# Attention softmax: the VectorE queue of a step is put into another order

## The chip, the cores and the metric

The kernel runs on one core of a Trainium2 chip. The metric is the device time of one execution of the whole program in microseconds (us); less is better. TensorE multiplies, VectorE (DVE in the profile) does reductions and elementwise work and reads PSUM, ScalarE (ACT) evaluates functions and copies out of PSUM, GpSimd (POOL) does elementwise work in SBUF alone. Each engine works through its own queue in program order, and the queues meet at semaphores.

## The reference, cut to what matters

The program computes six layers on a residual stream x of 8 x 256 tokens x 128 channels: a small graph of FFN nodes, the attention layer, the FFN graph again, a mixture of experts, a state-space layer and a second mixture. Only attention is touched by the change:

```python
xn = (x - mu) / jnp.sqrt(var + 1e-05) * ln_gamma + ln_beta
q, k, v = jnp.split(xn @ w_qkv, 3, axis=-1)      # 16 heads of 64
def rotate(t):
    t1, t2 = (t[..., :half], t[..., half:])
    return jnp.concatenate([t1 * cos - t2 * sin, t2 * cos + t1 * sin], axis=-1)
qr, kr = (rotate(q), rotate(k))
scores = jnp.einsum('bhid,bhjd->bhij', qr, kr) * scale
probs = jax.nn.softmax(scores, axis=-1)
out = jnp.einsum('bhij,bhjd->bhid', probs, v)
out = out.transpose(0, 2, 1, 3).reshape(b, n, INNER)
return out @ w_out + b_out
```

## The kernel before

Attention (`attn_phase`) is cut into 32 units: 8 sequences (b) times 4 groups of four heads (p). A loop of 37 steps runs a software pipeline over them, the same loop in the queue of each engine. In step s, unit f = s is projected and rotated, unit m = s - 2 goes through scores and softmax, unit t = s - 3 through the transposes and the product with v, and unit o = s - 4 through the output projection and the addition to x. Step s - 5 names z, of which only the last group of a sequence matters: there `moments` takes mean and variance of the finished x, in one step of four.

TensorE's order in a step: `scores` (L843), transposes of heads 0 and 1 (`turn`, L855), `project_out` (L881), first projection (`project(f, 0)`, L817), transposes of heads 2 and 3, `values` (L828), second projection (`project(f, 1)`, L817 again), `context` (L871). The two projections share one PSUM bank, `proj`, so that `project(f, 1)` waits until VectorE has done `rotate(f, 0)`, and the next unit's `project(f, 0)` until `rotate(f, 1)` is done. Both are two multiplications of `proj` by the tables into `turned` (L920). `values` waits for `add(o)` (L960), which reads the same bank `vc`. The next step's `scores` waits for the fourth exponential (`pr_sb`), since that one reads the last of the score banks.

VectorE's softmax work: `row_max` is a reduction of one head's scores (L929), `negate` turns the maxima of two heads into the bias of the exponentials (L935), `invert` takes the reciprocal of the sums of two heads once their exponentials are done (L941), and `normalize` multiplies the four tiles of heads 0 and 1 (L948). GpSimd does the sums and differences of the rotation (`rot`, L1009 and L1011) and the multiplication of heads 2 and 3 (L1018), in the order first rotation, multiplication, second rotation; the multiplication waits for the second `invert`.

ScalarE's order in a step: two copies of transposes (`pt`, L1043), exponentials of heads 0 and 1 (L1058, two per head, each with a read of the sum), two more copies, the copy of v (L1084, waits for `values`), exponentials of heads 2 and 3, the copy of the context (L1050). The exponentials of heads 2 and 3 wait for `negate` of the second pair.

VectorE's order is written out by hand in the step loop that the diff changes. No planner and no DMA has a part in it.

Of the kernel before, what the change touches and what calls it, by code (L numbers as in the profile page):

```python
# [8 lines left out]
ALU = mybir.AluOpType  # L9
ACT = mybir.ActivationFunctionType  # L10
AX = mybir.AxisListType
# [731 lines left out]
QUADS = HA // 4  # L743
HALF = DA // 2
UNITS_A = B * QUADS
SOFT_LAG, TURN_LAG, PROJ_LAG = 2, 3, 4
# [12 lines left out]
def attn_unit(step, lag):  # L759

    return Unit(step - lag) if 0 <= step - lag < UNITS_A else None
# [16 lines left out]
def attn_phase(k, a):  # L778

    nc, d = k.nc, k.d  # L780
    wqk, wv, wo, rope, bo = a.wqk, a.wv, a.wo, a.rope, a.bo
    with ExitStack() as ctx:
# [3 lines left out]
        mx = k.sb("at_mx", [P, 2, 8], ctx)  # L786
# [8 lines left out]
        sc = [k.psum(f"at_sc{h}", [P, 2, N], ctx) for h in range(4)]  # L795
# [5 lines left out]
        s = {n: k.sem(f"at_{n}", ctx) for n in names}  # L801
# [110 lines left out]
        @block.vector  # L912
        def _(dve):
            def rotate(f, which):

                dve.wait_ge(s["proj_ps"], 2 * f.n + which + 1)
                if f.n:
                    dve.wait_ge(s["rot_sb"], 4 * f.n - 2 + 2 * which)
                for i in range(2):
                    last = nc.vector.tensor_tensor(turned[:, which, i, :, :], proj[:, :, :],  # L920
                                                   rope[:, i:i + 1, :].broadcast_to([P, 2, N]), ALU.mult)
                last.then_inc(s["rope_sb"], 1)

            def row_max(m, pair):

                if pair == 0:
                    dve.wait_ge(s["sc_ps"], m.n + 1)
                for h in (2 * pair, 2 * pair + 1):
                    last = nc.vector.tensor_reduce(mx[:, m.two, 2 * h:2 * h + 2], sc[h][:, :, :], AX.X, ALU.max)  # L929
                last.then_inc(s["mx_sb"], 1)  # L930

            def negate(m, pair):

                dve.wait_ge(s["mx_sb"], 2 * m.n + pair + 1)
                nc.vector.tensor_scalar(nmx[:, m.two, 4 * pair:4 * pair + 4], mx[:, m.two, 4 * pair:4 * pair + 4], -scale,  # L935
                                        None, ALU.mult).then_inc(s["nmx_sb"], 1)

            def invert(m, pair):

                dve.wait_ge(s["pr_sb"], 4 * m.n + 2 * pair + 2)  # L940
                nc.vector.reciprocal(rinv[:, m.two, 4 * pair:4 * pair + 4], rsum[:, m.two, 4 * pair:4 * pair + 4])\  # L941
                    .then_inc(s["rinv_sb"], 1)

            def normalize(m):

                dve.wait_ge(s["rinv_sb"], 2 * m.n + 1)
                for i in range(4):
                    last = nc.vector.tensor_scalar(pr[:, m.two, i, :], pr[:, m.two, i, :], rinv[:, m.two, i:i + 1],  # L948
                                                   None, ALU.mult)
                last.then_inc(s["pn01_sb"], 1)  # L950

            def add(o):

                dve.wait_ge(s["op_ps"], o.n + 1)
                if o.n:
                    dve.wait_ge(s["x_sb"], o.n)
                else:
                    dve.wait_ge(s["bias"], 1)
                xs = k.x[:, 2 * o.b:2 * o.b + 2, :]
                nc.vector.tensor_tensor(xs, xs, vc[:, 0, :].rearrange("p (t d) -> p t d", t=2), ALU.add)\  # L960
                    .then_inc(s["x_sb"], 1)

            def moments(b):

                dve.wait_ge(s["x_sb"], QUADS * (b + 1))
                for i in range(2):
                    nc.vector.bn_stats(stx[:, b % 2, i, :], k.x[:, 2 * b + i, :]).then_inc(s["stx_sb"], 1)
                for i in range(2):
                    dve.wait_ge(s["stx_sb"], 2 * b + i + 1)
                    nc.vector.bn_aggr(k.mv[:, 2 * b + i, :], stx[:, b % 2, i, :])  # L970

            front.invert(dve)
            for b in range(2):
                front.center(dve, b)
            dve.wait_ge(a.loaded, 16 * (len(a.loads) + 1))
            for step in steps:
                f, m, o = attn_unit(step, 0), attn_unit(step, SOFT_LAG), attn_unit(step, PROJ_LAG)
                if m:
                    row_max(m, 0)
                    negate(m, 0)  # L980
                    row_max(m, 1)
                if o:
                    add(o)
                z = attn_unit(step, PROJ_LAG + 1)
                if z and z.p == QUADS - 1:
                    moments(z.b)
                if m:
                    negate(m, 1)
                if f:
                    rotate(f, 0)  # L990
                if m:
                    invert(m, 0)
                if f:
                    rotate(f, 1)
                if step == 0:
                    for b in range(2, B):
                        front.center(dve, b)
                if m:
                    invert(m, 1)
                    normalize(m)  # L1000

        @block.gpsimd
        def _(pool):
# [1103 lines left out]
```

## Time and profile before

| | |
|---|---|
| runs, median of 3 | 2348.8 us (2347.6 to 2350.88) |
| profiled execution, time | 2348.22 us |
| its span | 2346.5 us |
| TensorE busy | 2108.6 us, 90% |
| VectorE busy | 1750.2 us, 75% |
| ScalarE busy | 1373.3 us, 59% |
| GpSimd busy | 997.3 us, 43% |
| attention, first scores to the last addition | 566.9 to 880 us |

The span is the time between the first and the last recorded instruction; the execution's own time is 1.7 us longer. Busy shares are means over all layers. For a change in one layer, the stretch of that layer is to be read, and there the length of a step, from one `scores` to the next.

### The profile page before, as it was taken

The page shows a single profiled execution, that of the slowest core. Times are in us where ns is not written, and L with a number is a line of the kernel's source. Part 1 is how long each engine was busy: PE and PEld are TensorE (multiplying, and loading weights), DVE is VectorE, ACT ScalarE, POOL GpSimd, SP SyncE. Part 2 cuts the span into 40 slices and gives each one's busy share as a digit, 9 for nine tenths or more (in the row PEclk, how much of TensorE's full clock was granted, in tenths as well). Part 3 has the DMA queues.
Part 4 walks back from the last instruction along what each step waited for, and adds up shares of the span by engine and source line. Part 5 has one row for each costly group of instructions (what it writes and reads, how often), then busy time and mean ns, then how long its engine had stood idle before and what let it go on. Part 6 is the DMA issues. An engine that isn't in the chain of part 4 may idle for free. (4 is left out here: it accounts for less than half of the span.)

```text
span 2346.5 us, 41150 instructions
## 1 busy us (share of the span) xinstructions
PE 2108.6 (90%) x14740; PEld 1526.7 (65%) x14740; DVE 1750.2 (75%) x3007; ACT 1373.3 (59%) x2711; POOL 997.3 (43%) x1461
## 2 busy tenths in 40 slices
PE   4899999986999985999999979699999999999978
PEld 3566666654777763666666645486776776866745
DVE  5666666666777767666666665499999999999963
ACT  1566666674777762666666663467567576575433
POOL 2444444523776654444445403033343333333313
PEclk7899999997999996999999998899999999999979
DMA  5555555530000004455555504000000000000000
GB/s 164 128 137 132 136 137 135 132 73 1 2 1 2 2 1 107 131 133 134 133 138 133 132 25 178 1 1 1 1 1 1 1 1 1 1 1 1 1 14 18
DMA packets 147459, 144.77 MB, mean 62 GB/s; under 512 B 14272, under 2 KB 107072, under 8 KB 146368
## 3 DMA queue, kind: packets, MB, share of 16 engines
q1 hardware_dynamic: 147264, 142.22, 23.0%
q8 instruction: 116, 1.90, 0.4%
q14 instruction: 79, 0.65, 0.1%
HBM read 93.94 MB, written 38.80 MB: 57 GB/s over the span
## 5 line engine op out<-in xcount | busy, mean ns | idle before, releaser
L604 DVE TENSOR_REDUCE sb_f_mx<-ps_f_s 128x2 f32<-128x512 f32 x768 | 504.6, 687 | 286.7 <-PE ps_f_s L360 285.6
L534 ACT ACTIVATE sb_f_pt<-ps_f_t 128x1024 f32<-128x1024 f32 x384 | 390.6, 1020 | 91.6 <-PE ps_f_t L377 91.2
L1959 POOL TENSOR_TENSOR sb_mb_h<-sb_mb_h 128x512 f32<-128x512 f32 x128 | 165.9, 1317 | 490.6 <-DVE sb_mb_h L1819 490.6
L360 PE MATMUL ps_f_s<-sb_f_stack 96*128 96x256 bf16 x1536 | 287.2, 279 | 54.8 <-DVE sb_f_mx L604 27.2
L1814 DVE TENSOR_TENSOR_SCAN sb_mb_h<-sb_mb_da,sb_mb_h 128x1024 f32<-128x1024 f32 x128 | 291.0, 2312 | 2.1 <-ACT sb_mb_da L1678 2.1
L1527 PE MATMUL ps_mb_f<-sb_mb_fc,sb_mb_cw 128*128 128x256 f32 x1280 | 285.3, 380 | 2.0 <-ACT sb_mb_fc L1692 2.0
L1527 PEld LDWEIGHTS ps_mb_f<-sb_mb_fc,sb_mb_cw 128*128 128x128 f32 x1280 | 240.2, 190 | 37.2 <-ACT sb_mb_fc L1692 4.3
L1678 ACT ACTIVATE sb_mb_da<-sb_mb_dl,sb_mb_an 128x255 f32<-128x255 f32 x512 | 211.4, 495 | 54.9 <-DVE sb_mb_h L1814 39.4
L712 POOL CAST sb_f_parts<-sb_f_qf 128x512 bf16<-128x512 f32 x96 | 58.5, 609 | 425.2 <-ACT sb_f_qf L561 425.2
L377 PE MATMUL ps_f_t<-sb_f_stack 128*128 128x256 bf16 x1536 | 234.7, 275 | 1.5 <-ACT sb_f_pt L534 1.5
L360 PEld LDWEIGHTS ps_f_s<-sb_f_stack 96*128 96x128 bf16 x1536 | 140.9, 99 | 105.2 <-DVE sb_f_mx L604 66.9
L433 PE MATMUL ps_f_a<-sb_f_pt,sb_f_v 128*32 128x256 f32 x3072 | 186.6, 384 | 0.0
L377 PEld LDWEIGHTS ps_f_t<-sb_f_stack 128*128 128x128 bf16 x1536 | 142.3, 98 | 59.7 <-issue 38.7
L545 ACT ACTIVATE sb_f_cs<-ps_f_a 128x512 f32<-128x512 f32 x96 | 57.3, 597 | 179.7 <-PE ps_f_a L433 179.7
L1819 DVE TENSOR_TENSOR sb_mb_h<-sb_mb_h,ps_mb_c 128x1024 f32<-128x1024 f32 x128 | 148.6, 1200 | 2.6 <-PE ps_mb_c L1563 2.6
L1807 DVE TENSOR_TENSOR sb_mb_h<-ps_mb_b,sb_mb_dx 128x1024 f32<-128x1024 f32 x128 | 150.0, 1211 | 0.5
L433 PEld LDWEIGHTS ps_f_a<-sb_f_pt,sb_f_v 128*32 128x32 f32 x3072 | 90.4, 110 | 82.6 <-issue 33.5
L1018 POOL TENSOR_SCALAR sb_at_pr<-sb_at_pr,sb_at_rinv 128x256 f32<-128x256 f32 x128 | 120.0, 952 | 50.2 <-DVE sb_at_rinv L941 50.2
L1058 ACT ACTIVATE sb_at_pr<-ps_at_sc,sb_at_nmx 128x256 f32<-128x256 f32 x256 | 118.3, 486 | 5.0 <-DVE sb_at_nmx L935 4.1
L716 POOL TENSOR_TENSOR sb_f_r<-sb_f_qf,sb_f_parts 128x512 f32<-128x512 f32 x96 | 112.5, 1172 | 7.7
L721 POOL TENSOR_TENSOR sb_f_parts<-sb_f_r,sb_f_parts 128x512 bf16<-128x512 f32 x96 | 111.8, 1164 | 7.7
L920 DVE TENSOR_TENSOR sb_at_turned<-ps_at_proj,sb_at_rope 128x512 f32<-128x512 f32 x128 | 82.2, 683 | 43.4 <-PE ps_at_proj L817 43.4
(256 smaller groups left out, 4209.9 us busy)
## 6 DMA issues: line engine op xcount, KB each, us to landing
f_scr<-sb_f_parts SPq DMA_DIRECT2D x96, 384.0 KB, 2.8
sb_f_stack<-f_scr SPq DMA_DIRECT2D x192, 192.0 KB, 3.1
sb_f_stack<-f_scr SPq DMA_DIRECT2D x192, 128.0 KB, 3.1
sb_f_stack<-f_scr SPq DMA_DIRECT2D x192, 64.0 KB, 3.3
sb_f_stack<-sb_f_mrow SPq DMA_DIRECT2D x96, 96.0 KB
sb_mb_cw<-in_cw SPq DMA_DIRECT2D x1, 5120.0 KB, 19.9
sb_m_w<-in_w SPq DMA_DIRECT2D x6, 256.0 KB, 3.1
sb_prep_weT<-in_weT SPq DMA_DIRECT2D x1, 1152.0 KB, 7.3
```

What stands on the lines that cost most here:

```text
L360: last = nc.tensor.matmul(s_bank[j % 2][:, h, :], stack[0:ROWS, a.n % STACKS, 0, g * GROUP + pair * 2 + h, half * P:(half + 1) * P], stack ...
L377: last = nc.tensor.matmul(t_bank[i % 2][:, h, :], stack[:, e.n % STACKS, 1, g * GROUP + h, half * P:(half + 1) * P], stack[:, e.n % STACKS ...
L433: last = nc.tensor.matmul(act_bank[h * SLOT:(h + 1) * SLOT, g * N:(g + 1) * N], v[:, u.two, half, g * GROUP + h, :], pt[:, u.two, g, half, ...
L534: nc.scalar.activation(pt[:, e.two, g, half, :, :], t_bank[i % 2][:, :, :], ACT.Exp).then_inc(s["pt_sb"], 1)
L604: nc.vector.tensor_reduce(mx[:, a.two, half, head:head + 2], s_bank[j % 2][:, :, :], AX.X, ALU.max)\
L1018: last = nc.gpsimd.tensor_scalar(pr[:, m.two, i, :], pr[:, m.two, i, :], rinv[:, m.two, i:i + 1], None, ALU.mult)
L1527: last = nc.tensor.matmul(f_bank[(1 + oc // 2) % 2][:, (oc % 2) * N:(oc % 2 + 1) * N], cw[:, ic, tap, oc * P:(oc + 1) * P], fc[:, ic, tap: ...
L1678: last = nc.scalar.activation(da[:, un % 2, c, i, 1:N], dl[:, m.parity, r, c, 1:N], ACT.Exp, scale=an[:, r, c, n:n + 1])
L1807: nc.vector.tensor_tensor(hb[:, c, :, :], b_bank[:, :, :], dx[:, m.parity, r, c:c + 1, :].broadcast_to([P, SG, N]), ALU.mult)\
L1814: nc.vector.tensor_tensor_scan(flat, da[:, un % 2, c, :, :].rearrange("p i n -> p (i n)"), flat, 0.0, ALU.mult, ALU.add).then_inc(s["scan_ ...
L1819: nc.vector.tensor_tensor(hb[:, c, :, :], hb[:, c, :, :], c_bank[:, :, :], ALU.mult).then_inc(s["hc_sb"], 1)
L1959: nc.gpsimd.tensor_tensor(hb[:, c, 0:2, :], hb[:, c, 0:2, :], hb[:, c, 2:4, :], ALU.add).then_inc(s["half_sb"], 1)
```

## The change

Maxima are now signalled one head at a time instead of one pair at a time, and the order of VectorE's queue in a step is another one. `add` and the first rotation come ahead of the fourth maximum; `invert` of the first pair, `normalize` and `invert` of the second pair come ahead of the second rotation; `moments` goes to the end of the step. The work and every other engine's queue stay as they are.

```diff
-            def row_max(m, pair):
-                if pair == 0:
+            def row_max(m, h):
+                if h == 0:
                     dve.wait_ge(s["sc_ps"], m.n + 1)
-                for h in (2 * pair, 2 * pair + 1):
-                    last = nc.vector.tensor_reduce(mx[:, m.two, 2 * h:2 * h + 2], sc[h][:, :, :], AX.X, ALU.max)
-                last.then_inc(s["mx_sb"], 1)
+                nc.vector.tensor_reduce(mx[:, m.two, 2 * h:2 * h + 2], sc[h][:, :, :], AX.X, ALU.max).then_inc(s["mx_sb"], 1)
 
             def negate(m, pair):
-                dve.wait_ge(s["mx_sb"], 2 * m.n + pair + 1)
+                dve.wait_ge(s["mx_sb"], 4 * m.n + 2 * pair + 2)
...
                 if m:
                     row_max(m, 0)
+                    row_max(m, 1)
                     negate(m, 0)
-                    row_max(m, 1)
+                    row_max(m, 2)
                 if o:
                     add(o)
-                z = attn_unit(step, PROJ_LAG + 1)
-                if z and z.p == QUADS - 1:
-                    moments(z.b)
-                if m:
-                    negate(m, 1)
                 if f:
                     rotate(f, 0)
                 if m:
+                    row_max(m, 3)
+                    negate(m, 1)
                     invert(m, 0)
+                    normalize(m)
+                    invert(m, 1)
                 if f:
                     rotate(f, 1)
                 if step == 0:
                     for b in range(2, B):
                         front.center(dve, b)
-                if m:
-                    invert(m, 1)
-                    normalize(m)
+                z = attn_unit(step, PROJ_LAG + 1)
+                if z and z.p == QUADS - 1:
+                    moments(z.b)
```

## Rows read from the trace of the kernel before

**Rows 1.** The page, busy time by engine.

```profile
PE 2108.6 (90%) x14740; PEld 1526.7 (65%) x14740; DVE 1750.2 (75%) x3007; ACT 1373.3 (59%) x2711; POOL 997.3 (43%) x1461
```

**Rows 2.** Busy time by stretch: start:end, length, engines (count), granted clock, DMA.

```profile
574.85:586.48 11.63, 11.54 (x76) 8.87 (x76) 8.58 (x20) 6.30 (x21) 6.44 (x8) 0.74 0.01 2
586.48:853.18 266.70, 263.51 (x2355) 203.55 (x2353) 207.96 (x503) 193.69 (x616) 183.77 (x225) 1.00 0.01 2
...
624.07:634.00 9.93, 9.47 (x89) 7.27 (x87) 7.88 (x23) 6.90 (x22) 6.87 (x9) 1.00 0.01 2
709.97:719.83 9.86, 9.72 (x87) 7.29 (x85) 7.86 (x18) 6.90 (x22) 6.37 (x9) 1.00 0.00 0
```

**Rows 3.** Waits between 586 and 853 us: total us, times, longest.

```profile
PEld ps_at_proj L817 <- DVE sb_at_turned L920: 12.2, 28, 0.9
```

**Rows 4.** Timeline of TensorE, one ordinary step: start, us, count, idle before.

```profile
690.69 2.01 PE L843 MATMUL ps_at_sc<-sb_at_rot 32*128 32x256 f32 x32
...
694.46 1.03 PE L817 MATMUL ps_at_proj<-sb_xT,sb_at_wqk 128*128 128x256 f32 x4
695.32 1.04 PE L855 MATMUL ps_at_tp<-sb_ident,sb_at_pr 128*128 128x128 f32 x8
696.20 1.03 PE L828 MATMUL ps_at_vc<-sb_at_wv,sb_xT 128*128 128x256 f32 x4
697.10 1.13 PE L817 MATMUL ps_at_proj<-sb_xT,sb_at_wqk 128*128 128x256 f32 x4
698.16 1.95 PE L871 MATMUL ps_at_vc<-sb_at_pt,sb_at_v 128*64 128x256 f32 x16
700.04 0.50 PE L843 MATMUL ps_at_sc<-sb_at_rot 32*128 32x256 f32 x4
```

**Rows 5.** Timeline of VectorE, the same step.

```profile
692.77 1.29 DVE L929 TENSOR_REDUCE sb_at_mx<-ps_at_sc 128x2 f32<-128x512 f32 x2 [0.54 <-PE ps_at_sc L843]
...
694.17 1.28 DVE L929 TENSOR_REDUCE sb_at_mx<-ps_at_sc 128x2 f32<-128x512 f32 x2
...
695.77 1.28 DVE L920 TENSOR_TENSOR sb_at_turned<-ps_at_proj,sb_at_rope 128x512 f32<-128x512 f32 x2
...
699.81 1.73 DVE L948 TENSOR_SCALAR sb_at_pr<-sb_at_pr,sb_at_rinv 128x256 f32<-128x256 f32 x4
```

**Rows 6.** Timeline of VectorE, ScalarE and GpSimd, the step before it.

```profile
681.26 3.83 POOL L1018 TENSOR_SCALAR sb_at_pr<-sb_at_pr,sb_at_rinv 128x256 f32<-128x256 f32 x4 [1.45 <-DVE sb_at_rinv L941]
...
684.71 0.41 DVE L935 TENSOR_SCALAR sb_at_nmx<-sb_at_mx 128x4 f32<-128x4 f32 x1
...
685.16 0.47 ACT L1058 ACTIVATE sb_at_pr<-ps_at_sc,sb_at_nmx 128x256 f32<-128x256 f32 x1
...
687.92 0.63 ACT L1084 ACTIVATE sb_at_v<-ps_at_vc 128x512 f32<-128x512 f32 x1
...
690.10 0.27 ACT L1058 ACTIVATION_READ_ACCUMULATOR sb_at_pr<-ps_at_sc,sb_at_nmx 128x1 f32 x1
```

**Rows 7.** Timeline of GpSimd, multiplication of the ordinary step.

```profile
690.68 3.65 POOL L1018 TENSOR_SCALAR sb_at_pr<-sb_at_pr,sb_at_rinv 128x256 f32<-128x256 f32 x4 [1.49 <-DVE sb_at_rinv L941]
```

**Rows 8.** Timeline of all engines, a step with moments.

```profile
705.04 0.48 DVE L967 BATCH_NORM_STATS2 sb_at_stx<-sb_x 128x6 f32<-128x128 f32 x2
...
705.44 0.30 DVE L970 BATCH_NORM_AGGREGATE sb_mv<-sb_at_stx 128x2 f32<-128x6 f32 x2
...
707.03 1.13 PE L817 MATMUL ps_at_proj<-sb_xT,sb_at_wqk 128*128 128x256 f32 x4 [0.47 <-DVE sb_at_turned L920]
```

**Rows 9.** Timeline of VectorE and GpSimd, the long step after it.

```profile
713.30 0.72 POOL L1009 TENSOR_TENSOR sb_at_rot<-sb_at_turned 128x256 f32<-128x256 f32 x1
713.37 0.68 DVE L935 TENSOR_SCALAR sb_at_nmx<-sb_at_mx 128x4 f32<-128x4 f32 x1
...
713.98 0.72 POOL L1011 TENSOR_TENSOR sb_at_rot<-sb_at_turned 128x256 f32<-128x256 f32 x1
```

**Rows 10.** Line L948 over the whole span: shortest, median and longest ns.

```profile
L948 DVE TENSOR_SCALAR sb_at_pr<-sb_at_pr,sb_at_rinv x128: 322/488/569, 575.5 to 871.3; 128x256 f32<-128x256 f32 x128
```

## The prediction

> **What bounds the kernel now.** I read the page first: TensorE is busy for 90% of the span [rows 1], a mean over six layers. The change touches attention alone, so I cut that layer into stretches. Between 586.48 and 853.18 us lie 28 full steps in 266.70 us, 9.525 us each, at full granted clock (1.00, the 2.4 GHz level), with TensorE busy for 263.51 us [rows 2]. So TensorE sets the pace and there is little to win; what there is must be time in which it waits. Among the waits of that stretch, the one for VectorE is the weight load of the second projection behind the first rotation, 12.2 us in 28 waits [rows 3]. Part of that is only the loss of a load that is otherwise done ahead, so the wait is no price by itself. The price is read from the length of the steps.
>
> An ordinary step takes 700.04 - 690.69 = 9.35 us [rows 4]. The six steps of this stretch that hold `moments` take about 9.93 [rows 2], as in the one whose second projection starts after 0.47 us of idle time [rows 8]. Two more take 9.86 and 9.93, the first of them shown [rows 2]. The sum agrees: 28 x 9.35 = 261.8, eight long steps add 8 x 0.57 = 4.6, and 0.3 us is left for the first step and odd ones.
>
> Why are two of them long? In one, the small `negate` of VectorE starts at 713.37, just after GpSimd began a rotation at 713.30, and is over at 714.05, 0.03 us after that rotation's end at 714.02, though the next one of GpSimd begins at 713.98 [rows 9]. It lasts 0.68 there for four columns, as long as a rotation multiplication of 512 columns, half of 1.28 [rows 5]. So this operation stands still while GpSimd works, and gets in between two operations of GpSimd. The rest of VectorE's queue moves back with it.
>
> **The new step, part by part.** All times below count from the start of `scores`.
>
> TensorE first. `values` starts at 696.20 - 690.69 = 5.51. It should be followed by the second projection at the distance that the first projection has to its successor, 695.32 - 694.46 = 0.86, so at 6.37. The second projection lasts 1.13 where it waited and 1.03 where the first did not [rows 4]; its successor comes 1.06 after it now, so I expect 0.96 without the wait, and `context` at 7.33. `scores` follows 700.04 - 698.16 = 1.88 later: 9.21 us. I take this reading of the 0.10 since both groups are four matmuls of one shape; the other end is that 1.06 stays, which gives 9.31.
>
> Does VectorE let it? The maxima start at 692.77 - 690.69 = 2.08, two take 1.29, the third begins at 3.48 and lasts about 0.68 [rows 5]; `add` follows to 4.50. The first rotation now stands behind the first projection, which ends at 3.77 + 1.03 = 4.80. It runs from 4.84 to 6.12, against 695.77 + 1.28 - 690.69 = 6.36 now [rows 5]. That is ahead of the 6.37 at which TensorE is ready, with 0.25 to spare. In steps with `moments` it came 0.58 later still, since its two statistics and two aggregates take 705.04 to 705.74 [rows 8]; that is gone too.
>
> The fourth maximum runs from about 6.04 to 6.72, and `negate` of the second pair arrives at 6.75. GpSimd starts its rotation about 0.07 behind VectorE's, at 6.19 to 6.91, 0.72 for each operation [rows 9], so `negate` stands still until 6.94. ScalarE doesn't mind: it copies v from 687.92 - 681.31 = 6.61, `scores` of that step being at 681.31, and starts the third head's exponentials about 7.07.
>
> `invert` of the first pair and `normalize` come next, partly behind GpSimd's second rotation operation, which ends at 7.60. A multiplication of `normalize` took 0.32 at best and 0.49 in the median [rows 10], all but the first of each four beside GpSimd's own; four took 1.73 [rows 5]. So they end between 8.7 and 9.3. I take 8.7, since GpSimd is idle then. `invert` of the second pair waits for the last exponential at about 9.06 anyway, so this costs nothing; at the upper end it would cost 0.2 a step.
>
> What is behind `invert` now? The second rotation, 1.29 long, and `moments`. They end at about 10.5 and 11.2, or 1.3 and 1.9 in the next step. The next maxima can't start before 2.08, the next first projection before 3.77. GpSimd reads the second rotation only after its multiplications. So the move costs nothing either, with 0.2 to spare in the moments steps.
>
> **The next bound.** There is a ring through three engines. GpSimd's four multiplications end at 685.09; `negate` of the first pair, begun at 684.71, stands still until 685.12; ScalarE begins at 685.16 and is busy until the last read at 690.37; GpSimd begins again at 690.68 [rows 6, 7]. So: 0.07 + 5.21 + 0.31 + 3.65 = 9.24 us. Today the step is longer, and the ring is slack. If the step were shorter than 9.24, GpSimd would end later in each step, and the ring would take over. I take 9.24.
>
> The sum: 28 x 9.24 = 258.7 against 266.7, a gain of 8.0 us. Its bounds: 9.21 a step gives 8.8; 9.35, with the long steps alone removed, gives 4.9. The ends of the layer change little. In the first softmax step the second exponentials wait 0.3 us longer for the late fourth maximum; in the next one, 11.63 us long at a mean granted clock of 0.74 [rows 2], `negate` collides less and 0.4 comes back. In the last steps the second half of the multiplications on GpSimd decides, which stays. I put nothing for them. A slow-clock stretch that comes or goes there is worth up to 11.63 - 9.53 = 2.1 us, the difference to the next step.
>
> Against its own time the profiled execution would become 2348.22 - 8.0 = 2340.2; it lies 0.6 below the median, so the median would be 2340.8, say 2341.
>
> **A rule weighed.** The rows say that `negate` waits for the whole of GpSimd's rotation operation [rows 9], but that VectorE's four multiplications take 1.73 beside GpSimd's of 0.92 each, so they don't each wait for a whole one [rows 5, 7]. The Trainium skill ("SBUF — State Buffer", section "SBUF: two separate sides") says that VectorE in a two-port mode and GpSimd share a port pair by an exclusive lock for the whole instruction. The first trace observation agrees, the second doesn't. By the rule alone, `normalize` away from GpSimd's multiplications should also let those run sooner, and the ring would lose up to 0.1; I leave the sum as it is.
>
> **Rivals.** (A) TensorE's spacing of 1.06 stays or some 9.35 us pace has another cause: only the long steps shrink. Gain 4.9, time 2344. For it: six of the eight are plainly due to `moments`. Against: the second projection waits in every step.
>
> (B) The ring is longer than I have it: GpSimd's multiplications take 3.83 in the step before [rows 6], and if the second rotation beside them slows them so, the ring is 9.42. Then 28 x 9.42 = 263.8, gain 2.9, time 2346. For it: 3.83 occurs. Against: VectorE's multiplications ran beside it then, and the rotation reads PSUM.
>
> (C) The other side: `negate` of the second pair falls behind both rotation operations of GpSimd. It arrives at 6.75; GpSimd's second one begins about 6.87. If `negate` is late by more than 0.12, or is not let in between, it ends at 7.63, the exponentials run from 7.67 to 9.62, and `scores` follows about 0.15 later at 9.77: 28 x 9.77 = 273.6, 6.9 us slower, time 2356. Against it: in [rows 9] it was let in between with the same spacing.
>
> (D) The new order does nothing that counts: `invert`, now ahead of the second rotation, holds the queue by as much as the early rotation frees. It would need the maxima to start later than 2.08, thus 0.2 us more in moments steps and 0.75 in the others. Time 2348.
>
> **How the numbers follow.** The forecast, gain between 6.5 and 9, has a chance of 0.56; A 0.16; B 0.12; C 0.10; D 0.06. The time is the likeliest case's, 2341. Faster by over 0.2% means below 2344.1 (0.2% is about what a measurement of this kernel can tell from no change): the forecast, most of A and a little of B, 0.70. Slower: C, 0.10. The rest, 0.20, lies within. The likeliest case's own range is 2339 to 2343; with A and part of B, and 2 us for a clock stretch, the range is 2338 to 2347.
>
> **What the new profile should show.** Steps of about 9.24 us between 586 and 845, with and without `moments`; no idle time of TensorE ahead of the second projection; the first rotation starting right behind the first projection; the second `negate` over by 7.0; `normalize` over before the last exponential; GpSimd's multiplications ending at 3.8. The prediction is wrong if the second `negate` ends at 7.6, if ScalarE's last exponential moves back, or if the maxima start later than 2.1.

## The result, and the profile after

The changed kernel takes 0.9961 of the time before, with a 95% interval of 0.9945 to 0.9977: 0.2% to 0.6% faster. The medians over seven runs each are 2344.54 us and 2350.89 us; single runs of one kernel spread by 7 to 9 us. The medians differ by 6.4 us, the means (2343.1 and 2352.3 us, whose ratio is that 0.9961) by 9.2, so the gain is known only to within a few us. The first profiled execution went from 2348.22 to 2338.9 us, its span from 2346.5 to 2337.1 us.

Not all of these 9.4 us are the change's. From the first `scores` to the last aggregate of `moments`, attention went from 313.97 (566.86 to 880.83) to 306.10 us (569.08 to 875.18), 7.9 less. It began 2.2 us later, and what lies behind it became 3.7 us shorter. No instruction of either part was changed, and the later runs will show such stretches move by several us.

These are the stretch of 28 full steps, by the view of [rows 2] (start:end, length, busy TensorE, weight loads, VectorE, ScalarE, GpSimd with counts, granted clock, DMA), and one step that holds `moments`:

```profile
589.03:847.11 258.08, 258.08 (x2355) 208.63 (x2353) 210.78 (x502) 193.40 (x616) 179.71 (x224) 1.00 0.01 2
635.11:644.33 9.22, 9.22 (x87) 7.44 (x85) 8.01 (x23) 6.91 (x22) 6.41 (x8) 1.00 0.01 2
847.11:855.79 8.68, 6.81 (x75) 5.29 (x73) 5.79 (x17) 6.42 (x21) 5.01 (x6) 1.00 0.01 4
```

258.08 us against 266.70 [rows 2], and TensorE is busy in all of it. All 28 steps take 9.21 or 9.22 us, whether they hold `moments` or not. The wait of [rows 3] has left the list of waits. The third row is the first step without a new unit; it is longer than the 8.48 us of before, and the section on the prediction says why.

TensorE in one of these steps, to be held against [rows 4]:

```profile
690.42 2.01 PE L843 MATMUL ps_at_sc<-sb_at_rot 32*128 32x256 f32 x32
...
695.92 1.03 PE L828 MATMUL ps_at_vc<-sb_at_wv,sb_xT 128*128 128x256 f32 x4
696.79 1.03 PE L817 MATMUL ps_at_proj<-sb_xT,sb_at_wqk 128*128 128x256 f32 x4
697.76 1.95 PE L871 MATMUL ps_at_vc<-sb_at_pt,sb_at_v 128*64 128x256 f32 x16
699.64 0.50 PE L843 MATMUL ps_at_sc<-sb_at_rot 32*128 32x256 f32 x4
```

The second projection follows `values` by 0.87 us and is followed after 0.97, against 0.90 and 1.06 [rows 4]. The two differences, 0.12 us, are what an ordinary step lost, but for 0.01.

VectorE in the same step, against [rows 5]:

```profile
693.82 0.36 DVE L933 TENSOR_SCALAR sb_at_nmx<-sb_at_mx 128x4 f32<-128x4 f32 x1
...
695.25 1.29 DVE L920 TENSOR_TENSOR sb_at_turned<-ps_at_proj,sb_at_rope 128x512 f32<-128x512 f32 x2 [0.34 <-PE ps_at_proj L817]
696.46 0.68 DVE L928 TENSOR_REDUCE sb_at_mx<-ps_at_sc 128x2 f32<-128x512 f32 x1
697.17 0.20 DVE L933 TENSOR_SCALAR sb_at_nmx<-sb_at_mx 128x4 f32<-128x4 f32 x1
697.29 0.17 DVE L939 RECIPROCAL sb_at_rinv<-sb_at_rsum 128x4 f32<-128x4 f32 x1
697.49 1.49 DVE L946 TENSOR_SCALAR sb_at_pr<-sb_at_pr,sb_at_rinv 128x256 f32<-128x256 f32 x4
699.48 0.18 DVE L939 RECIPROCAL sb_at_rinv<-sb_at_rsum 128x4 f32<-128x4 f32 x1 [0.50 <-ACT sb_at_pr L1056]
```

VectorE now idles 0.34 us ahead of the first rotation, which waits for TensorE instead of keeping it waiting. It also idles 0.50 us ahead of the second `invert`, which waits for ScalarE. GpSimd around that step, against [rows 6, 7, 9]:

```profile
690.53 3.63 POOL L1016 TENSOR_SCALAR sb_at_pr<-sb_at_pr,sb_at_rinv 128x256 f32<-128x256 f32 x4 [1.72 <-DVE sb_at_rinv L939]
...
696.62 0.73 POOL L1007 TENSOR_TENSOR sb_at_rot<-sb_at_turned 128x256 f32<-128x256 f32 x1 [1.07 <-DVE sb_at_turned L920]
697.30 0.73 POOL L1009 TENSOR_TENSOR sb_at_rot<-sb_at_turned 128x256 f32<-128x256 f32 x1
```

Its multiplications end at 694.16, and the first `negate` at 694.18. Its rotation operation ends at 697.35, and the second `negate` at 697.37. Both stand still behind GpSimd, as forecast.

### The profile page after: what moved, and what is told of

The parts are those of the page before. It is cut to its first block and busy times, and to the rows that moved or that the text cites. A ratio compares the mean times of both kernels' runs of the same rounds, so it can differ in the third digit from the quotient of the medians.

```text
span 2337.1 us, 41150 instructions
## 1 busy us (share of the span) xinstructions
PE 2104.3 (90%) x14740; PEld 1530.6 (65%) x14740; DVE 1752.7 (75%) x3007; ACT 1374.4 (59%) x2711; POOL 992.2 (42%) x1461
## 5 line engine op out<-in xcount | busy, mean ns | idle before, releaser
L1960 POOL TENSOR_TENSOR sb_mb_h<-sb_mb_h 128x256 f32<-128x256 f32 x128 | 108.1, 866 | 0.0
```

## The experiments

All ratios are against the kernel before. "28 steps" is the length of the stretch that takes 266.70 us before. The runs came in three groups of four, in the order of the rows, each on one chip and with runs of the kernel before beside them. A ratio whose interval holds 1 shows no change: that is so for `moments` last alone, whose gain is seen in its profile only.

| kernel | ratio, 95% interval | 28 steps, us |
|---|---|---|
| first half alone | 0.9957 (0.9944 to 0.9970) | 258.26 |
| second half alone | 1.0049 (1.0033 to 1.0064) | 275.87 |
| moments last alone | 0.9987 (0.9973 to 1.0002) | 262.72 |
| all, moments at the old place | 0.9955 (0.9940 to 0.9970) | 258.44 |
| negate late, 3 operations | 0.9969 (0.9956 to 0.9983) | 257.80 |
| half an output projection | 0.9979 (0.9963 to 0.9995) | 257.67 |
| the same, no negate | 0.9925 (0.9907 to 0.9943) | 252.56 |
| all, no negate | 0.9965 (0.9949 to 0.9980) | 257.67 |
| negate late, 5 operations | 1.0018 (1.0003 to 1.0033) | 272.95 |
| candidate | 0.9940 (0.9922 to 0.9958) | 257.66 |
| second half alone, no negate | 0.9959 (0.9944 to 0.9974) | 260.52 |
| changed kernel again | 0.9965 (0.9954 to 0.9977) | 257.72 |

### The first half alone

```diff
                 if o:
                     add(o)
                 z = attn_unit(step, PROJ_LAG + 1)
                 if z and z.p == QUADS - 1:
                     moments(z.b)
-                if m:
-                    negate(m, 1)
                 if f:
                     rotate(f, 0)
                 if m:
+                    row_max(m, 3)
+                    negate(m, 1)
                     invert(m, 0)
                 if f:
                     rotate(f, 1)
...
                     invert(m, 1)
                     normalize(m)
```

> Only the first half of the change: the addition and the first rotation ahead of the fourth maximum. The second rotation stays ahead of the second invert and of normalize, and the moments stay ahead of the first rotation. If the ring of GpSimd's multiplications, the first negate and ScalarE is what stands next behind TensorE, normalize beside those multiplications slows them again (3.65 to 3.83 us in place of 3.63) and the ordinary step is 9.24 to 9.42 us; gain against the kernel before 3 to 8 us. If the early rotation is all that counts, the ordinary step is 9.22 as in the changed kernel and the moments steps about 9.36, gain 7.5 to 8 us.

Its windows row, and GpSimd and VectorE in an ordinary step that starts at 614.62:

```profile
587.01:845.27 258.26, 258.26 (x2355) 205.84 (x2353) 210.80 (x502) 193.61 (x616) 184.77 (x224) 1.00 0.01 2
```

```profile
614.72 3.84 POOL L1017 TENSOR_SCALAR sb_at_pr<-sb_at_pr,sb_at_rinv 128x256 f32<-128x256 f32 x4 [1.69 <-DVE sb_at_rinv L939]
```

```profile
618.02 0.17 DVE L933 TENSOR_SCALAR sb_at_nmx<-sb_at_mx 128x4 f32<-128x4 f32 x1
```

Ordinary steps take 9.20 to 9.24 us, moments steps 9.28. So this half is the whole gain, and the first of the two expectations, the ring at 9.24 to 9.42, is refuted here. GpSimd does take 3.84 us, but `negate` isn't held until its end at 618.56: it begins at 618.02 and is over at 618.19. The fourth multiplication, 0.93 long, began at 617.63, 0.39 us before. In the changed kernel it began at 694.16 - 0.93 = 693.23, 0.59 us before `negate`, which is held there. So a multiplication on GpSimd holds `negate` only if it is well under way.

The kernel before shows it too. In its step at 843.76 the fourth multiplication begins at 846.66 (843.75 + 3.84 - 0.93), and `negate`, 0.50 us behind, gets through:

```profile
843.75 3.84 POOL L1018 TENSOR_SCALAR sb_at_pr<-sb_at_pr,sb_at_rinv 128x256 f32<-128x256 f32 x4 [1.49 <-DVE sb_at_rinv L941]
```

```profile
847.16 0.17 DVE L935 TENSOR_SCALAR sb_at_nmx<-sb_at_mx 128x4 f32<-128x4 f32 x1
```

In the step of [rows 6] it came 0.53 us behind and was held. Over all profiles that have `negate`, it got through in each of the 37 cases in which it came 0.31 us to just under 0.50 us after the start of a multiplication. It was held to the end in each of the 230 in which it came just over 0.50 us to 0.75 us after. What changes inside the multiplication at that point is not shown.

### The second half alone

```diff
                 if m:
                     invert(m, 0)
+                    normalize(m)
+                    invert(m, 1)
                 if f:
                     rotate(f, 1)
...
-                if m:
-                    invert(m, 1)
-                    normalize(m)
```

> Only the second half: invert, normalize and the second invert ahead of the second rotation; the fourth maximum, the moments and the second negate stay ahead of the first rotation. If the gain comes from the first rotation being early for TensorE, ordinary steps stay at 9.35 us and the six moments steps at about 9.9, and the gain is 0 to 1.5 us (the two steps that are long without moments may go). If normalize beside GpSimd was the real cost, ordinary steps fall below 9.30 and the gain is 3 us or more.

Neither expectation fits: it is slower than before. The windows row, and three engines in a step that starts at 643.34, the second after the first moments step:

```profile
586.47:862.34 275.87, 269.21 (x2354) 203.94 (x2352) 232.06 (x502) 193.50 (x616) 181.09 (x225) 1.00 0.01 1
```

```profile
646.72 0.73 POOL L1008 TENSOR_TENSOR sb_at_rot<-sb_at_turned 128x256 f32<-128x256 f32 x1
646.74 0.73 DVE L933 TENSOR_SCALAR sb_at_nmx<-sb_at_mx 128x4 f32<-128x4 f32 x1
...
647.38 1.28 DVE L928 TENSOR_REDUCE sb_at_mx<-ps_at_sc 128x2 f32<-128x512 f32 x2
...
648.58 0.40 DVE L958 TENSOR_TENSOR sb_x<-sb_x,ps_at_vc 128x256 f32<-128x256 f32 x1
...
648.98 1.28 DVE L920 TENSOR_TENSOR sb_at_turned<-ps_at_proj,sb_at_rope 128x512 f32<-128x512 f32 x2
```

`negate` is held by GpSimd's rotation operation for all of its length, and the third and fourth maximum, `add` and the first rotation move back by 0.56 us. This is what made two steps long before [rows 9]; here it starts behind the first step with `moments` and keeps itself going. The lengths of the first 13 of the 28 steps are 9.35 four times, 9.94 with `moments`, 9.53, 9.91, 9.91, 10.49 with `moments`, 9.53, 9.91, 9.91 and 10.50 with `moments`. In a step of 9.91 us, GpSimd's multiplications start at 9.69 and last 3.62, so they end at 3.40 of the next step, and the rotation operation begins at 3.38, just ahead of the 3.40 at which `negate` comes. The next step is long for that reason, and so on.

### The second half alone, without negate

`negate` goes: the rotation tables are scaled once by the square root of the score scale, so that the scores come out scaled, and the reductions write negative maxima themselves. Each head's exponentials then wait for their own maximum alone.

```diff
+            nc.vector.tensor_scalar(rope[:, :, :], rope[:, :, :], scale ** 0.5, None, ALU.mult).then_inc(s["mx_sb"], 1)
+            dve.wait_ge(s["mx_sb"], 1)
             for step in steps:
...
-                nc.vector.tensor_reduce(mx[:, m.two, 2 * h:2 * h + 2], sc[h][:, :, :], AX.X, ALU.max).then_inc(s["mx_sb"], 1)
+                nc.vector.tensor_reduce(nmx[:, m.two, 2 * h:2 * h + 2], sc[h][:, :, :], AX.X, ALU.max, negate=True)\
+                    .then_inc(s["nmx_sb"], 1)
...
-                act.wait_ge(s["nmx_sb"], 2 * m.n + h // 2 + 1)
+                act.wait_ge(s["nmx_sb"], 4 * m.n + h + 1)
...
-                    last = nc.scalar.activation(pr[:, m.two, i, :], sc[h][:, i % 2, :], ACT.Exp, scale=scale,
+                    last = nc.scalar.activation(pr[:, m.two, i, :], sc[h][:, i % 2, :], ACT.Exp,
```

> The second half of the change alone, as in the run that became slower, but without negate. If that run was slow because GpSimd's rotation operation, early in the step, holds up the first negate of the next step, all steps that were 9.5 to 9.9 us without moments return to 9.35 us and the six steps with moments to 9.93; the program is some 12 to 16 us faster than that run, 0 to 4 us faster than before. If something else in the order made them long (the second rotation behind the second invert), they stay at 9.5 to 9.9.

```profile
587.87:848.39 260.52, 259.26 (x2355) 205.22 (x2353) 216.05 (x446) 193.40 (x616) 181.36 (x224) 1.00 0.01 2
```

The long steps are gone: 9.20 us for each ordinary step, 9.68 with `moments`. So the held `negate` was their cause, not the second rotation behind `invert`. They are shorter than the 9.35 that I expected, since taking both negates out of the queue lets even the old order reach the first rotation as soon as its projection is done (4.83 us). In steps without `moments`, leaving `negate` out thus gives as much as the early rotation does.

### Moments last, and moments early

The first takes the old order and moves `moments` alone to the end of the step; the second takes the changed kernel and puts them back.

```diff
@@ moments last
                 if o:
                     add(o)
-                z = attn_unit(step, PROJ_LAG + 1)
-                if z and z.p == QUADS - 1:
-                    moments(z.b)
...
                     normalize(m)
+                z = attn_unit(step, PROJ_LAG + 1)
+                if z and z.p == QUADS - 1:
+                    moments(z.b)
```

> Only the moments move, to the end of the step, behind normalize; the rest is the order of before. If the moments steps were long only since the moments delay the first rotation, they fall from 9.93 to about 9.45 us (the moments now end at 2.2 us of the next step and its maxima start 0.1 late) and ordinary steps stay at 9.35: gain 3 to 4.5 us. If they cost their 0.6 us wherever they stand, the gain is 0.

> The changed kernel with the moments back ahead of the first rotation. VectorE now has idle time there, so the rotation ends at about 6.40 us in place of 6.12, and the second negate at about 7.22, the step with moments being 9.28 to 9.36 us: 0.4 to 0.9 us more than the changed kernel in all, gain about 7.8 us. If the old place costs its full 0.58 us in six steps, it is 3.5 us slower than the changed kernel.

The windows rows, first of the one and then of the other:

```profile
587.39:850.11 262.72, 262.65 (x2355) 203.55 (x2353) 206.42 (x502) 193.39 (x616) 184.79 (x225) 1.00 0.01 2
```

```profile
588.94:847.38 258.44, 258.44 (x2354) 207.25 (x2352) 210.18 (x502) 193.83 (x616) 179.59 (x224) 1.00 0.01 2
```

In the old order the move takes 4.0 us off, inside the 3 to 4.5 expected; steps behind the first are 9.35 to 9.42, and none is long any more. Two of those that are gone had been long without `moments` [rows 9]. The program's ratio, 0.9987 (0.9973 to 1.0002), doesn't show the gain by itself. In the new order the place costs 0.06 us in each of six steps (9.28 in place of 9.22), since VectorE has 0.34 us of idle time there, as expected. The two moves are two ways to the same gain, and don't add up.

### The second negate made late

```diff
                     row_max(m, 3)
-                    negate(m, 1)
                     invert(m, 0)
+                    spare(m)          # three, then five reciprocals of rsum into a spare tile
+                    negate(m, 1)
                     normalize(m)
```

> The changed kernel with the second negate made about 0.2 to 0.4 us late: it stands behind the first invert and three further reciprocals of the same four columns, which are written to a spare tile and read by nothing. If rival C has the price right, negate now arrives after GpSimd's second rotation operation has begun (6.88 us), stands still until 7.62, and the step becomes about 9.75 us: some 15 us slower than the changed kernel, 6 slower than before. If negate doesn't stand still behind that operation, it ends at about 7.2 and the step is 9.3 us, 2.5 us slower than the changed kernel.

> As the run with three further reciprocals, but with five, so that the second negate reaches the head of the queue at about 7.1 us instead of 6.91, well behind the start of GpSimd's second rotation operation at 6.88. If a wait of rival C exists, it now ends at about 7.65, the third head's exponentials start at 7.7 and the step is about 9.77 us: 28 times 0.55, 15 us slower than the changed kernel. If negate of four columns gets through, it ends at 7.25 and the step is about 9.35 us, 4 us slower.

With three, VectorE and then GpSimd in the step that starts at 662.26:

```profile
669.17 0.14 DVE L934 TENSOR_SCALAR sb_at_nmx<-sb_at_mx 128x4 f32<-128x4 f32 x1
```

```profile
668.46 0.73 POOL L1014 TENSOR_TENSOR sb_at_rot<-sb_at_turned 128x256 f32<-128x256 f32 x1 [1.08 <-DVE sb_at_turned L921]
669.15 0.75 POOL L1016 TENSOR_TENSOR sb_at_rot<-sb_at_turned 128x256 f32<-128x256 f32 x1
```

With five, VectorE, GpSimd and ScalarE in the step that starts at 666.39, and its windows row:

```profile
673.43 0.60 DVE L934 TENSOR_SCALAR sb_at_nmx<-sb_at_mx 128x4 f32<-128x4 f32 x1
```

```profile
673.27 0.73 POOL L1016 TENSOR_TENSOR sb_at_rot<-sb_at_turned 128x256 f32<-128x256 f32 x1
```

```profile
674.06 0.48 ACT L1063 ACTIVATE sb_at_pr<-ps_at_sc,sb_at_nmx 128x256 f32<-128x256 f32 x1 [0.42 <-DVE sb_at_nmx L934]
```

```profile
588.41:861.36 272.95, 261.50 (x2355) 213.81 (x2353) 216.25 (x642) 193.56 (x617) 179.94 (x224) 1.00 0.01 2
```

With three operations `negate` begins 0.02 us after GpSimd's second rotation operation by the record, is through in 0.14, and nothing changes: 257.80 us, which neither expectation had. With five it begins 0.16 us after, is held to 674.03, and all 28 steps take 9.74 to 9.76 us. Rival C's price was 9.77. In these two runs the wait sets in not at 6.87 but between 6.91 and 7.03 us of the step, with `negate` at 6.75 in the changed kernel.

How near is safe is open all the same. The kernel before holds a counterexample, in the second softmax step, which begins at 574.85:

```profile
580.02 0.77 DVE L935 TENSOR_SCALAR sb_at_nmx<-sb_at_mx 128x4 f32<-128x4 f32 x1
```

```profile
579.36 0.72 POOL L1009 TENSOR_TENSOR sb_at_rot<-sb_at_turned 128x256 f32<-128x256 f32 x1
580.04 0.72 POOL L1011 TENSOR_TENSOR sb_at_rot<-sb_at_turned 128x256 f32<-128x256 f32 x1
```

This `negate` came 0.66 us after the first rotation operation began, 0.02 us before the second, and was held behind both. In the changed kernel it comes 0.55 us after (697.17 and 696.62), only 0.11 us earlier. In the second half alone, one that came 0.02 us after a rotation operation (646.74 and 646.72) was held too; there a multiplication ran before.

### Less work for TensorE, with and without negate

```diff
-                    for pair in range(2):
-                        last = nc.tensor.matmul(..., cx[:, o.two, pair, ...], wo[:, 2 * o.p + pair, :], start=pair == 0, stop=pair == 1)
+                    last = nc.tensor.matmul(..., cx[:, o.two, 0, ...], wo[:, 2 * o.p, :], start=True, stop=True)
```

> The changed kernel with half of the output projection left out (the second pair of heads of each unit isn't projected), which takes 0.43 us of TensorE's work out of each step: TensorE alone could do a step in 8.79 us. If the ring of GpSimd's multiplications, the first negate and ScalarE is already as long as TensorE's step, the step stays at 9.20 to 9.22 us and the whole program gains under 1 us on the changed kernel. If the ring has slack, the step falls to 8.8 to 9.0 us, 6 to 12 us less than the changed kernel.

> The same kernel with half of the output projection left out, and without negate: the rotation tables are scaled once by the square root of the score scale, the reductions write negative maxima themselves, and the exponentials read them. Nothing in the ring then stands still behind GpSimd. If the port wait of negate closes the ring, the exponentials start at about 3.45 us in place of 3.80 and the step falls to 8.8 to 8.95 us, 7 to 12 us less than with negate. If ScalarE alone sets 9.2, nothing changes.

TensorE with negate, in the step that starts at 662.75, and the windows rows of the two:

```profile
668.67 1.03 PE L817 MATMUL ps_at_proj<-sb_xT,sb_at_wqk 128*128 128x256 f32 x4
670.07 1.95 PE L871 MATMUL ps_at_vc<-sb_at_pt,sb_at_v 128*64 128x256 f32 x16 [0.37 <-ACT sb_at_v L1081]
```

```profile
589.13:846.80 257.67, 247.14 (x2243) 198.72 (x2241) 208.16 (x502) 193.11 (x616) 179.60 (x224) 1.00 0.01 1
```

```profile
588.16:840.72 252.56, 247.10 (x2243) 198.91 (x2241) 207.22 (x446) 190.00 (x616) 179.81 (x224) 1.00 0.01 2
```

With 0.43 us less to do in each step, TensorE idles and the step stays at 9.20: 257.67 us. Something else is just as long. Without `negate` it falls to 9.02, so the held `negate` is a part of that ring. The link to TensorE isn't the one I had named: `context` waits 0.37 us for the copy of v, which stands behind the exponentials of heads 0 and 1 in ScalarE's queue. I expected 8.8 to 8.95. The exponentials start at 3.60 without negate, not 3.45, since ScalarE copies transposes until then; from there to 8.82 it has no gap. That makes its queue the likely next bound, but no run tests it. Both kernels leave out a part of the output projection, so they serve to read the step and nothing else.

### The changed kernel without negate, a candidate, and the changed kernel again

The candidate takes the first half, `moments` last and no negate; `normalize` stays behind the second rotation.

```python
                 if m:
                     row_max(m, 0)
                     row_max(m, 1)
                     row_max(m, 2)
                 if o:
                     add(o)
                 if f:
                     rotate(f, 0)
                 if m:
                     row_max(m, 3)
                     invert(m, 0)
                 if f:
                     rotate(f, 1)
...
                 if m:
                     invert(m, 1)
                     normalize(m)
                 z = attn_unit(step, PROJ_LAG + 1)
                 if z and z.p == QUADS - 1:
                     moments(z.b)
```

> The changed kernel with its whole output projection, without negate in the same way. If TensorE's own work is the floor, full steps stay at 9.21 us, and only the first and last steps of the layer, in which softmax is on the path, give back 0.5 to 1.5 us. If the ring was the bound, the step falls below 9.15.

> A candidate for a better version: only the early addition and first rotation, second rotation and then the second invert and normalize as before, moments last, and no negate (scaled rotation tables, reductions that write negative maxima, one signal for each head). Full steps should be 9.20 us, with moments too, the first two softmax steps 7.2 and 10.7 us and the last 8.48: 2 to 3 us less than the changed kernel in attention, unless a stretch at the lower clock level takes it away; 10 to 12 us less than before.

> The changed kernel once more, on the same chip as the candidate: 7 to 10 us less than before, full steps of 9.22 us.

Windows rows of the candidate, the first softmax steps and the full ones, and the first softmax steps of the changed kernel:

```profile
567.82:575.01 7.19, 5.06 (x45) 3.68 (x45) 5.87 (x11) 4.60 (x18) 4.29 (x7) 1.00 0.00 1
575.01:585.71 10.70, 10.05 (x76) 8.06 (x77) 7.20 (x17) 6.20 (x21) 6.63 (x8) 0.84 0.01 2
585.71:843.37 257.66, 257.66 (x2354) 205.69 (x2352) 204.88 (x446) 193.42 (x616) 184.22 (x224) 1.00 0.01 2
```

```profile
569.08:577.39 8.31, 5.07 (x46) 3.69 (x45) 7.01 (x17) 4.71 (x18) 4.31 (x7) 0.93 0.00 1
577.39:589.03 11.64, 11.11 (x77) 8.86 (x77) 7.13 (x18) 6.31 (x21) 6.43 (x8) 0.76 0.01 2
```

Without negate, 28 steps take 257.67 us, 9.20 each, with TensorE busy throughout, and with less work for TensorE it was 9.02: 9.20 is TensorE's floor. What is won by leaving `negate` out lies in the first two softmax steps, 2.06 us in sum. In the first, 1.12 us are won since a head's exponentials start as soon as its own maximum is there, at 2.80 us of the step in place of 3.61. In the second, 0.94 us are won, about the 0.88 by which its first transposes are shorter. Over that step the mean granted clock is 0.84 in place of 0.76, and the transposes no longer fall into the low stretch. All four kernels without `negate` took 10.69 or 10.70 us there; why the clock is low for less time is not shown. The transposes in the changed kernel and in the candidate:

```profile
581.12 1.97 PE L855 MATMUL ps_at_tp<-sb_ident,sb_at_pr 128*128 128x128 f32 x8
```

```profile
578.62 1.09 PE L854 MATMUL ps_at_tp<-sb_ident,sb_at_pr 128*128 128x128 f32 x8
```

Attention takes 303.4 us in the candidate's profile, 2.7 less than in the first profile of the changed kernel and 4.0 less than in that of its run in this group. Of the 4.0, 1.7 are a low clock at the end of attention in the latter, shown in the last section. The candidate's ratio is 0.9940, the changed kernel's in the same group 0.9965. The intervals overlap by a little, so that the candidate beats the kernel before is shown, and that it beats the changed one is likely. Whether the candidate needs the early rotation is untested: without `negate`, the old place of the first rotation gave ordinary steps of 9.20 too.

The changed kernel without negate and without the other edits saw none of that gain in the total (0.9965) and little in its attention (305.8 us against 306.1). In its last 21.80 us TensorE was granted 0.81 on average, against 1.00 for the same stretch before:

```profile
850.84:872.64 21.80, 15.65 (x122) 11.47 (x120) 6.61 (x22) 9.64 (x27) 7.24 (x8) 0.81 0.00 0
```

## Why the prediction was right, and where it was off

**The pace.** TensorE's wait for the first rotation was the loss, and an ordinary step could fall to 9.21: right, measured 9.21 to 9.22. The 0.10 us that I took from a single difference, 1.03 against 1.13, was there: the second projection takes 1.03 now. Rival A, under which only the long steps shrink, is out.

**The moments.** 0.58 us in each of six steps came back. The move alone brings 4.0 us in the old order, the two steps that were long without `moments` included, but in the new order the old place would have cost only 0.4. I had put the gain on the move; the early rotation makes it nearly needless.

**The queue behind the second invert.** The second rotation ended 1.20 us into the next step, `moments` at 1.81, the maxima began at 2.08. Forecast: 1.3, 1.9, 2.08. Rival D is out.

**The ring.** It was forecast at 9.24 and is 9.20 to 9.22: with TensorE relieved the step stays, without negate it falls. So I named the right next bound. Its role was overrated, since TensorE's own floor is as long. Its rule was too simple: the first half alone has slower multiplications on GpSimd and no slower steps, as a multiplication doesn't hold `negate` all the time. Rival B is out: with the second rotation beside them, the multiplications took 3.63 us, not 3.83. What slows them is `normalize` beside them (3.84 in the first half alone).

**Normalize.** The forecast said that its early place costs nothing, and counted no gain for it. In the changed kernel that holds: it ended at 8.56 us of the step, where 8.7 was forecast. What I missed is how little it takes to turn it into a loss: in steps of 9.53 us and more, GpSimd's rotation operation lands on `negate`, and the second half alone is 0.5% slower than before. The first half protects it by keeping steps at 9.22, in which GpSimd's rotation operation begins at 3.70, 0.30 us behind `negate`. The two long steps of before were this mechanism, as I had read from [rows 9].

**Rival C.** The price was right to 0.02 us a step. The distance, 0.12 us in the forecast, isn't settled: a `negate` that came 0.16 us later did no harm in the run with three reciprocals, but one in the kernel before was held where 0.11 us later would put it. The forecast, which called on [rows 9] alone for being let in between, had not seen that one.

**The sum.** 28 steps: forecast 258.7, measured 258.08. The ends were put at nothing, and they cost 0.7 us: the first softmax step became 8.31 in place of 7.98 us, the last but one 8.68 in place of 8.48, and the last one and what follows 19.39 in place of 19.18. The first is the late second `negate` (5.99 us of the step in place of 4.79), the 0.3 us that the forecast had named. The 0.4 that was to come back in the second softmax step did not: `negate` was held there no more, 0.17 us long in place of 0.76, but the step took 11.64 us as against 11.63, and the first exponentials started at 6.23 us in place of 6.22. In the last two, `negate` is now held behind GpSimd's multiplications, which end at 3.74 and 3.79, and the exponentials start 0.20 and 0.25 us later. The forecast had left that out. The forecast's 8.0 us for the layer is 7.9 in the profile. The median of the runs after is 3.5 us above the 2341 forecast, within the range; the runs of before, seven now, have risen by 2.1 us over the three that the forecast stood on.

## What to carry to other kernels

When one engine is the bound, look for the queue that keeps it waiting and ask what stands ahead of the awaited instruction without need; moving an addition and a rotation ahead of one maximum (with its `negate`) gave the whole gain here. A four-column operation can be as dear as one of 512 columns if it has to wait for another engine's operation, so work out at which time of the step it comes and what runs then, in long steps too. Test the halves of a reordering apart: one can be the whole gain, and the other harmless only in its company.

## What was not expected of the hardware

A rotation operation on GpSimd (two SBUF inputs) holds VectorE's `negate` for its whole 0.72 us. A multiplication by a column there (0.92 us) does so only in part: `negate` got through when it came up to 0.50 us after one began, and was held when it came later. Between two rotation operations, a `negate` mostly gets in: it did so even 0.02 us after the record of the second had begun, in the run with three reciprocals, but once, 0.02 us before it, it did not. 0.16 us after was too late. The Trainium skill ("SBUF — State Buffer", section "SBUF: two separate sides") says that the lock lasts for the whole instruction: the rotation operations agree, the multiplications don't.

Without any change in their code, stretches of the program differ by several us between profiles. What lies behind attention took 1462.0 and 1466.7 us in the two profiles of the changed kernel. Attention's last stretch took 19.40 and 21.07 us in the same two, at mean granted clocks of 0.91 and 0.92. What counts there is where the low clock falls. These are the last product with v in the first and in the second profile:

```profile
870.18 1.95 PE L871 MATMUL ps_at_vc<-sb_at_pt,sb_at_v 128*64 128x256 f32 x16 [0.74 <-ACT sb_at_pt L1041]
```

```profile
873.54 3.63 PE L871 MATMUL ps_at_vc<-sb_at_pt,sb_at_v 128*64 128x256 f32 x16 [0.74 <-ACT sb_at_pt L1041]
```

The second ran at a granted clock of 0.53, mostly the 1.2 GHz level, and everything behind it waited, 1.68 us longer. In the first profile the clock was low one product earlier (862.60 us, 3.35 long), while the next work waited for GpSimd's multiplications anyway, and it cost nothing that shows. For a gain of 8 us in 2350, one profile's step length is a sharper measure than the program's time.
